# One change in four places of a fused attention and feed-forward kernel: convolution tiles, order of the attention's small products, composition schedule, seam

## The chip, the cores and the metric

The kernel runs on one core of one Trainium2 chip. It is written engine by engine (TensorE, VectorE, ScalarE, GpSimd and the DMA queues), with semaphores between them. The metric is the device time in microseconds, a median of runs. In the profile TensorE is PE (its weight loads PEld), VectorE DVE, ScalarE ACT, GpSimd POOL, SyncE SP.

## The reference, cut to what matters

The input has 8 sequences of 1024 tokens with 256 channels, all fp32. It goes through an attention encoder with a residual and a layer norm, then through a composed feed-forward part with a residual and a layer norm:

```
h = gelu(conv1d_grouped(x^T, conv1_w (1024,1,5), groups=256))      # 4 hidden channels each
h = conv1d_grouped(h, conv2_w (256,4,5), groups=256)^T
h = layernorm(h + x)
for i in range(4):                                                # 4 layers
    q = gelu(h Wq + bq) + 0.21;  k = gelu(h Wk + bk) + 0.21;  v = h Wv + bv
    q_r, k_r = rope(q), rope(k);  z = 1 / (q . mean(k))            # 16 heads of 16
    h = layernorm(q_r (k_r^T v / n) * z + h)
f = gelu(h W1 + b1) W2 + b2;  a = layernorm(f + h);  x = layernorm(x + a)
W1', W2' = sum over 32 chosen primitives of weight * A_k B_k       # top 32 of 64, softmax
out = layernorm(x + gelu_tanh(x W1') W2')
```

## The kernel before, in words

**Convolution (`conv_phase`, lines 57 to 376).** Four pairs of sequences times 8 channel groups are 32 steps. In step n TensorE runs `conv1(n)`, then `to_tokens(n - 2)` (transposes), then `conv2(n - 1)`. `conv1` (line 241) holds 32 fp32 products: 2 taps x 4 output slots `s` x 4 row groups `j`, each with 32 rows and 32 columns of the array and 512 moving columns; row group j writes PSUM bank `hid_ps[(4n + j) % 6]`, slot s its partitions 32s to 32s+31. Slots 0 and 1 take tap `second`, slots 2 and 3 tap `1 - second`. `conv2` (line 253) holds 8 products of 128 rows and 32 columns. ScalarE applies gelu (line 300), GpSimd copies edges (lines 185 to 187) and normalises an earlier pair, VectorE adds bias and input (line 322), keeps the turned rows (line 329) and measures them (`measure`). `prep` folds layer norm gains into the projection weights and biases: `prep.tensor` makes bias rows, `prep.tensor_columns` turns them into columns after ScalarE's `scalar_rows`, and `prep.vector_biases` finishes them. The last pair is normalised later, by `conv.last`, inside the first attention units.

**Attention (`attention_phase`).** 8 sequences x 4 layers are 32 units; unit n works on lane n % 4. TensorE's list for a unit, in order: `key_value(n-1)` (line 891, 128 rows by 32 columns), `project(n,0,"k",0)` (six fp32r products of 128x512), `turn_u(n,1)` (line 834, transposes of the second token half), `turn_kv(n-1)` (line 899, one product with the matrix `rot`), three more key projections, `turn_k` twice (line 854), `outputs(n-1)` (line 917, 32x32 tiles), `turn_k` twice, four query projections, `values` for four pairs of token tiles into `big[0..3]`, `turn_u(n+1,0)`, `denominators(n)` (line 876). What `turn_u` makes goes through ScalarE (`hT_hi`, line 956) and VectorE (`hT_lo`, line 1059), and the projections of that half wait for both. Projections, turned keys, denominators and key_value share four PSUM banks, `ring`, handed on in the order of `TURN`; `emptied_by` names the semaphore at which a bank comes free. GpSimd's list for a unit is `residual(n)` (it waits for `turn_u(n,1)`), an `invert` of an earlier unit, four `sum_k` and three rotations of q. VectorE copies the rotated kv (line 1145, `copy_turned`), measures unit n-2, rotates keys and finishes unit n-1.

**Composition (`compose_phase`).** 32 pairs of primitives ("duos", 16 per weight) are summed in PSUM. For pair n ScalarE makes the high parts (lines 1774, 1775), VectorE the low parts (lines 1804, 1806), TensorE multiplies. Three pairs are buffered (`SPLIT`), six raw loads (`RAW`). Between the pairs ScalarE and VectorE finish the last three attention units by a table written out by hand: `FINISH` (VectorE), `UNITS_AT` (ScalarE: four `unit` activations, before some of them `spread`, lines 1004 and 1005, after which GpSimd's `invert`, lines 797 and 799, runs), `FIRST_AT` (the first feed-forward weights), `TAKE_AT` (the finished weight 1 out of PSUM), `BIAS_AT`. The feed-forward part that follows (`ffn_phase`) is long and is not edited but for one more parameter.

Of the kernel before, what the change touches and what calls it, by code (L numbers as in the profile page):

```python
# [14 lines left out]
P = 128  # L15
# [28 lines left out]
def conv_phase(nc, x, bands1, bands2, conv1_b, conv2_b, eye, u0, comp, tri, w_col, picks, prep, keep, place, sems, stack,  # L44
# [5 lines left out]
    S = 4  # L50
# [13 lines left out]
    with ctx:  # L64
# [159 lines left out]

        def tensor(e, first):
            w = Waits(e)

            def conv1(n):
                l, cp = n // CP % 2, n % CP
                w.wait_ge(d_x[l][part_of(cp)], 16 * (n // CP // 2 + 1))  # L230
                w.wait_ge(d_band1[part_of(cp)], 2 * 16 if part_of(cp) else 16)

                for second in range(2):
                    for s in range(S):
                        k = second if s < 2 else 1 - second
                        for j in range(ROWS):
                            r = slice(32 * j, 32 * j + 32)
                            out = hid_of(n, j)[32 * s:32 * s + 32, :].rearrange("p (b g) -> p b g", b=2)
                            src = xs[l][r, cp, k:k + COLS].rearrange("p (b g) -> p b g", b=2)
                            w.wait_ge(s_hidden, ROWS * n + j - HID + 1)  # L240
                            m = e.matmul(out[:, :, second:], band1[r, cp, k, s, :], src[:, :, second:], start=not second,  # L241
                                         stop=bool(second))
                            if second and s == S - 1:
# [12 lines left out]

            def to_tokens(n):
                w.wait_ge(d_eye, 16)
                w.wait_ge(rank.s_v, rank.ROW + 1)
                w.wait_ge(s_convT, n + 1)  # L260
                w.wait_ge(s_y, n)
                for t in range(2 * MT):
                    m = e.transpose(back_ps[:, t, :], convT[:, n % 2, t * P:(t + 1) * P], identity[:, :])
                m.then_inc(s_back, 1)

            for n in range(STEPS + LAG):
                if n < STEPS:
                    conv1(n)
                if n == STEPS + LAG - 1:

                    w.wait_ge(s_hidden, ROWS * STEPS)
                    first()
                    prep.tensor(e)
                if 0 <= n - LAG < STEPS:
                    to_tokens(n - LAG)
                if 0 <= n - 1 < STEPS:
                    conv2(n - 1)
                if n == 1:
                    rank.tensor(e)
            prep.tensor_columns(e, identity)  # L280

# [32 lines left out]
        def vector(e, first):  # L314
# [17 lines left out]
            for n in range(STEPS + LAG):  # L332
# [3 lines left out]
                if n == STEPS + LAG - 1:  # L336
                    first()
                if 0 <= n - LAG < STEPS:
                    keep_rows(n - LAG)
# [5 lines left out]
                for layer in prep.due(n, 1):  # L345
                    prep.vector(e, layer)
            prep.vector_biases(e)

# [254 lines left out]
def attention_phase(nc, u_in, u_out, T, H, w_split, bias_qk, bias_v, keep, place, sems, stack, d_u0, d_u4, prefetch,  # L603
# [21 lines left out]
    with ctx:  # L625
# [64 lines left out]
        ring_of = lambda n, kind, b: ring[turn_of(n, kind, b) % RING]  # L690
        emptied_by = {"k": (s_gk, 4), "kt": (s_ks, 4), "q": (s_gq, 4), "den": (s_z, 1), "kv": (s_kvr, 1)}

# [123 lines left out]
        def tensor(e, then):  # L816
# [79 lines left out]
            def turn_kv(n):  # L896
                w.wait_ge(d_consts, 3 * 16)
                w.wait_ge(s_kvw, n + 1)
                e.matmul(ring_of(n, "kv", 0)[:, 2 * P:2 * P + CB * D], rot[:, :], kv[:, :, :].rearrange("p c n -> p (c n)"),
                         start=True, stop=True).then_inc(s_rot, 1)  # L900
# [18 lines left out]

            conv.tensor(e, lambda: turn_u(0, 0))  # L920
            for n in range(UNITS):
                if n >= 1:
                    key_value(n - 1)
                project(n, 0, "k", 0)
                turn_u(n, 1)
                if n >= 1:
                    turn_kv(n - 1)
                project(n, 0, "k", 1)
                project(n, 1, "k", 0)
                project(n, 1, "k", 1)  # L930
                turn_k(n, 0)
                turn_k(n, 1)
# [17 lines left out]
        def scalar(e, then):  # L950
# [87 lines left out]
            def last(g):  # L1038

                n = UNITS - 3 + g // 2  # L1040
                if g % 2 == 0 and n > UNITS - 3:
                    spread(n)
                for o in range(4 * (g % 2), 4 * (g % 2) + 4):
# [6 lines left out]

            then(e, last)

        def vector(e, then):
# [88 lines left out]
            def copy_turned(n):  # L1142
                w.wait_ge(s_rot, n + 1)
                w.wait_ge(s_out, n)
                e.tensor_copy(kv_rot[:, :, :].rearrange("p c n -> p (c n)"),
                              ring_of(n, "kv", 0)[:, 2 * P:2 * P + CB * D]).then_inc(s_kvr, 1)

# [10 lines left out]
            for n in range(UNITS):  # L1158
# [3 lines left out]
                split_u(n, 1)  # L1162
                if n >= 1:
                    copy_turned(n - 1)
                if n >= 2:
                    measure(n - 2, 0)
                    measure(n - 2, 1)
                if n == 0:
                    conv.last.vector(e, w, 0)
                    conv.last.vector(e, w, 1)  # L1170
                rotate_k(n, 0)
                k_mean(n)
                for u in range(1, DUOS):
                    if n == 0:
                        conv.last.vector(e, w, u + 1)
                    rotate_k(n, u)
# [5 lines left out]
                if n == 0:  # L1182
                    for half_group in range(5, 2 * conv.last.groups):
                        conv.last.vector(e, w, half_group)
# [25 lines left out]
def ffn_phase(nc, x, u_in, out, w1, b1, w2, rows2, comp, identity, w_col, picks, place, sems, before, early,  # L1210
# [12 lines left out]
    with ctx:  # L1223
# [238 lines left out]

        def scalar(e, last):
            w = Waits(e)
# [15 lines left out]

            compose.scalar(e, last, lambda: split_a(0, 0, 0))
            w.wait_ge(s_w_lo, 2)
# [194 lines left out]
def compose_phase(nc, up, down, comp, w_col, picks, place, sems, before, first, early, d_early):  # L1677
# [8 lines left out]
    with ctx:  # L1686
# [18 lines left out]
        FINISH = {2: 0, 4: 1, 5: 2, 6: 3, 7: 4, 9: 5, 10: 6, 11: 7, 12: 8, 13: 9, 15: 10}  # L1705
        UNITS_AT = {3: 0, 5: 1, 8: 2, 10: 3, 16: 4, 17: 5}

        FIRST_AT = {20: 0, 24: 1}
        TAKE_AT = DUOS + 6
        BIAS_AT = DUOS + 9  # L1710
        ROWS_AT = len(duos) - 3
# [50 lines left out]

        def scalar(e, last, rows):
            w = Waits(e)
# [19 lines left out]
            for n in range(len(duos)):  # L1784
                prepare(n)
                if n in UNITS_AT:
                    last(UNITS_AT[n])
                if n in FIRST_AT:
                    wait_free(w, before.free["all"])
                    first.scalar(e, FIRST_AT[n])  # L1790
# [266 lines left out]
```

## Time and profile before

| | us |
|---|---|
| runs, median (lowest to highest) | 1863.13 (1861.23 to 1863.57) |
| profiled execution, its own time | 1859.66 |
| its span | 1857.9 |

| engine | busy us | share of the span |
|---|---|---|
| PE | 1832.2 | 99% |
| PEld | 1528.6 | 82% |
| DVE | 1416.6 | 76% |
| ACT | 934.3 | 50% |
| POOL | 1011.6 | 54% |

The convolution fills about the first 163 us, the attention units the time to 1009.7, the composition that to 1109.9, the feed-forward part the rest. Matmuls are pipelined and overlap, so the time between the starts of two groups of products says more of TensorE than its busy share does. The granted clock is 0.998 of full speed over the span.

### The profile page before, as it was taken

Reading aid. Unit: us, or ns where it says so; the run is one execution under the profiler, and the core shown is the slowest. Engines: PE = TensorE matmul, PEld = TensorE weight load, DVE = VectorE, ACT = ScalarE, POOL = GpSimd, SP = SyncE. Lnnn points to the kernel's source line nnn. Section 1 sums busy time; section 2 is a strip of 40 time slices with the busy share of each in tenths; the row PEclk is TensorE's granted clock in tenths of the full one; section 3 lists DMA queues with packets and bytes.
Section 4 is the critical chain, followed back from the end, with each engine's and each line's share of the span. In section 5 each row is a group of like instructions: output and inputs, shape, how many; then the busy total and the mean of one; then the engine's idle time right before and its main releaser. Section 6 shows DMA issues by size and latency. Waiting matters only on the chain.

```text
span 1857.9 us, 50038 instructions
## 1 busy us (share of the span) xinstructions
PE 1832.2 (99%) x21188; PEld 1528.6 (82%) x21188; DVE 1416.6 (76%) x3329; ACT 934.3 (50%) x1741; POOL 1011.6 (54%) x775
## 2 busy tenths in 40 slices
PE   8999999999999999999999999999999999999998
PEld 2334888888888888888887799999999999999998
DVE  3556788888888888888887767777777777777777
ACT  4554667766676667766676653232323232323231
POOL 1455999899999999899996112222222222222221
PEclk9999999999999999999999999999999999999999
DMA  8354120010102110010104940010101010101000
GB/s 291 131 207 184 56 80 17 3 36 2 36 2 104 64 56 11 2 36 2 59 2 134 308 153 32 26 44 26 44 26 44 26 44 26 44 26 42 28 12 24
DMA packets 25249, 115.62 MB, mean 62 GB/s; under 512 B 4481, under 2 KB 5441, under 8 KB 19905
## 3 DMA queue, kind: packets, MB, share of 16 engines
q1 hardware_dynamic: 21104, 89.69, 13.7%
q0 software_dynamic: 1152, 12.58, 1.9%
q10 hardware_dynamic: 2768, 10.15, 1.4%
q8 instruction: 166, 2.72, 0.6%
q14 instruction: 59, 0.48, 0.1%
HBM read 80.95 MB, written 31.46 MB: 61 GB/s over the span
## 4 chain that ended last, share of the span: by engine, by line
PE 96%; DVE 2%; ACT 1%; issue 0%; DMA 0%; POOL 0%; SPq 0%; ACTq 0%; DVEq 0%; POOLq 0%
PE bankC L34 13%; PE bankC L33 13%; PE bankC L32 13%; PE ring L32 7%; PE ring L34 6%; PE ring L33 6%; PE big L917 5%; PE hid_ps L241 4%; PE big L34 3%; PE big L32 3%; PE big L33 3%; PE conv_ps L253 3%; PE ring L854 3%; PE big L834 3%; PE ring L891 2%; PE ring L876 2%
## 5 line engine op out<-in xcount | busy, mean ns | idle before, releaser
L32 PE MATMUL bankC<-down_hi,act_hi 128*128 128x256 f32 x1024 | 291.4, 285 | 0.0
L34 PE MATMUL bankC<-down_hi,act_lo 128*128 128x256 f32 x1024 | 289.6, 283 | 0.0
L33 PE MATMUL bankC<-down_lo,act_hi 128*128 128x256 f32 x1024 | 288.6, 282 | 0.0
L1553 DVE TENSOR_TENSOR act_lo<-gel,act_hi 128x512 fp32r<-128x512 f32 x256 | 210.9, 824 | 8.7
L34 PE MATMUL bankC<-aT_hi,up_lo 128*128 128x512 f32 x512 | 199.7, 390 | 0.0
L33 PE MATMUL bankC<-aT_lo,up_hi 128*128 128x512 f32 x512 | 199.5, 390 | 0.0
L32 PE MATMUL bankC<-aT_hi,up_hi 128*128 128x512 f32 x512 | 199.4, 389 | 0.0
L32 PEld LDWEIGHTS bankC<-down_hi,act_hi 128*128 128x128 f32 x1024 | 193.8, 189 | 1.2
L33 PEld LDWEIGHTS bankC<-down_lo,act_hi 128*128 128x128 f32 x1024 | 193.2, 189 | 1.4
L1507 POOL TENSOR_TENSOR hC<-hC,vecC 128x1024 f32<-128x1024 f32 x16 | 38.5, 2404 | 284.5 <-PE turn L1406 284.5
L34 PEld LDWEIGHTS bankC<-down_hi,act_lo 128*128 128x128 f32 x1024 | 193.2, 189 | 0.0
L1513 POOL TENSOR_TENSOR rstdC<-var_epsC,minus_halfC 128x4 f32<-128x4 f32 x47 | 52.8, 1123 | 254.1 <-DVE var_epsC L1578 254.1
L1059 DVE TENSOR_TENSOR hT_lo<-big,hT_hi 128x512 fp32r<-128x512 f32 x128 | 82.4, 686 | 109.0 <-ACT hT_hi L956 109.0
L762 POOL TENSOR_TENSOR kr<-kr,kc 128x512 f32<-128x512 f32 x128 | 161.7, 1297 | 0.0
L1478 ACT ACTIVATE gel<-bankC,b1s 128x512 f32<-128x512 f32 x128 | 88.4, 690 | 140.5 <-PE bankC L34 140.4
L1478 ACT ACTIVATE gel<-bankC 128x512 f32<-128x512 f32 x128 | 76.6, 599 | 155.5 <-PE bankC L34 155.5
L781 POOL TENSOR_TENSOR yB<-yB,shift 128x1024 f32<-128x1024 f32 x64 | 151.0, 2383 | 0.0
L1470 ACT ACTIVATE aT_hi<-turn 128x512 fp32r<-128x512 f32 x64 | 34.8, 596 | 217.1 <-PE turn L1406 217.1
L778 POOL TENSOR_TENSOR yB<-yB,gain 128x1024 f32<-128x1024 f32 x48 | 114.4, 2404 | 52.4 <-PE big L834 52.4
L996 ACT ACTIVATE yB<-yB,offset,rstdB 128x256 f32<-128x256 f32 x256 | 129.4, 588 | 5.5 <-POOL offset L799 5.5
L788 POOL TENSOR_TENSOR qc<-gT,cos_q 128x512 f32<-128x512 f32 x96 | 124.3, 1295 | 0.0
L789 POOL TENSOR_TENSOR qs<-gT,sin_q 128x512 f32<-128x512 f32 x96 | 123.6, 1288 | 0.0
(205 smaller groups left out, 5252.1 us busy)
## 6 DMA issues: line engine op xcount, KB each, us to landing
raw_late<-in_AB SPq DMA_DIRECT2D x30, 320.0 KB, 3.9
u<-hA SPq DMA_DIRECT2D x8, 1024.0 KB, 4.6
u_next<-u SPq DMA_DIRECT2D x8, 1024.0 KB, 4.8
hC<-u SPq DMA_DIRECT2D x16, 512.0 KB, 3.9
xC<-in_x SPq DMA_DIRECT2D x16, 512.0 KB, 4.8
out<-w_flat SPq DMA_DIRECT2D x15, 512.0 KB, 2.6
w_flat<-in_AB SPq DMA_DIRECT2D x22, 320.0 KB, 3.7
w_split<-w_parts ACTq DMA_DIRECT2D x4, 1536.0 KB, 5.3
```

The costliest lines, as they stand in the source:

```text
L32: e.matmul(out, wh, xh, start=start, stop=False)
L33: e.matmul(out, wh, xl, start=False, stop=False)
L34: return e.matmul(out, wl, xh, start=False, stop=stop)
L762: e.tensor_tensor(kr[:, u, :], kr[:, u, :], kc[:, u, :], ALU.add).then_inc(s_kr, 1)
L778: e.tensor_tensor(tiles(y, a), tiles(src, a), row(gain), ALU.mult).then_inc(s_mul, 1)
L781: e.tensor_tensor(tiles(y, a), tiles(y, a), row(shift), ALU.add).then_inc(s_res, 1)
L788: e.tensor_tensor(qc[:, db, cols], gT[:, db, cols], table_q(cos_q, db, x), ALU.mult)
L789: e.tensor_tensor(qs[:, db, cols], gT[:, db, cols], table_q(sin_q, db, x), ALU.mult).then_inc(s_qr, 1)
L917: m = e.matmul(out, wt[ch, db, :], quarter(q[ch, db, :], j), start=q is qc, stop=q is qs)
L996: e.activation(y[:, o, :], y[:, o, :], ACT.Identity, bias=offset[:, two, o:o + 1], scale=rstd[:, two, o:o + 1]).then_inc(s_unit, 1)
L1478: e.activation(gel[:, n % GEL, :], bank_of(i, k, s, fb)[:, :], ACT.Gelu if k == 0 else ACT.Gelu_apprx_tanh, bias=b1s[:, fb:fb + 1] if k == ...
L1553: e.tensor_tensor(a_lo[:, fb, :], g, a_hi[:, fb, :].bitcast(F32), ALU.subtract).then_inc(s_act_lo, 1)
```

## The change: what it does

- The first convolution uses 32x64 tiles: two neighbouring slots in one product of 64 columns, so 16 products per step instead of 32.
- In an attention unit `turn_u(n,1)` goes ahead of all four key projections and `turn_kv(n-1)` behind them. `turn_kv` writes `big[0]` instead of the ring bank, and that bank comes free at `s_kvw` instead of `s_kvr`. VectorE's `copy_turned` goes behind the two measurements of unit n-2.
- At the end of the convolution TensorE also turns the second half of unit 0 (`second`) and makes the bias columns before the last `to_tokens`; VectorE's biases move ahead of the last `keep_rows`. In unit 0 the measurements of the last convolution rows, but for the first two, go behind the rotated keys.
- In the composition `spread` is separate from `unit` (`SPREAD_AT`, after pairs 6 and 16; before, it ran after pairs 8 and 16 directly ahead of the units), the last two groups of units move from pairs 16 and 17 to 18 and 19, the first feed-forward weights from 20 and 24 to 22 and 25, take and bias one pair later.

```diff
-                    for s in range(S):
-                        k = second if s < 2 else 1 - second
+                    for half in range(2):
+                        k = 1 - second if half else second
                         for j in range(ROWS):
...
-                            out = hid_of(n, j)[32 * s:32 * s + 32, :].rearrange("p (b g) -> p b g", b=2)
+                            out = hid_of(n, j)[rows, :].rearrange("p (b g) -> p b g", b=2)
...
+                            bands = band1[r, cp, k, 2 * half:2 * half + 2, :].rearrange("p s c -> p (s c)")
...
-                            m = e.matmul(out[:, :, second:], band1[r, cp, k, s, :], src[:, :, second:], start=not second,
-                                         stop=bool(second))
+                            m = e.matmul(out[:, :, second:], bands, src[:, :, second:], start=not second, stop=bool(second))
@@ end of the convolution, TensorE
                     first()
                     prep.tensor(e)
+                    second()
+                    prep.tensor_columns(e, identity)
...
-            prep.tensor_columns(e, identity)
@@ end of the convolution, VectorE
                     first()
+                    prep.vector_biases(e)
...
-            prep.vector_biases(e)
@@ attention, ring and turn_kv
-        emptied_by = {..., "kv": (s_kvr, 1)}
+        emptied_by = {..., "kv": (s_kvw, 1)}
...
-                e.matmul(ring_of(n, "kv", 0)[:, 2 * P:2 * P + CB * D], rot[:, :], ...)
+                if n + 1 < UNITS:
+                    w.wait_ge(s_lo, 4 * (n + 1) + 2)
+                else:
+                    w.wait_ge(s_vs, 4 * n + 4)
+                e.matmul(big[0][:, 0:CB * D], rot[:, :], ...)
@@ attention, TensorE's list
-            conv.tensor(e, lambda: turn_u(0, 0))
+            conv.tensor(e, lambda: turn_u(0, 0), lambda: turn_u(0, 1))
             for n in range(UNITS):
                 if n >= 1:
                     key_value(n - 1)
+                    turn_u(n, 1)
                 project(n, 0, "k", 0)
-                turn_u(n, 1)
-                if n >= 1:
-                    turn_kv(n - 1)
                 project(n, 0, "k", 1)
                 project(n, 1, "k", 0)
                 project(n, 1, "k", 1)
+                if n >= 1:
+                    turn_kv(n - 1)
@@ attention, VectorE's list
-                if n >= 1:
-                    copy_turned(n - 1)
                 if n >= 2:
                     measure(n - 2, 0)
                     measure(n - 2, 1)
+                if n >= 1:
+                    copy_turned(n - 1)
...
-                    if n == 0:
-                        conv.last.vector(e, w, u + 1)
...
-                    for half_group in range(5, 2 * conv.last.groups):
+                    for half_group in range(2, 2 * conv.last.groups):
@@ composition
-        UNITS_AT = {3: 0, 5: 1, 8: 2, 10: 3, 16: 4, 17: 5}
-        FIRST_AT = {20: 0, 24: 1}
-        TAKE_AT = DUOS + 6
-        BIAS_AT = DUOS + 9
+        UNITS_AT = {3: 0, 5: 1, 8: 2, 10: 3, 18: 4, 19: 5}
+        SPREAD_AT = {6: 0, 16: 1}
+        FIRST_AT = {22: 0, 25: 1}
+        TAKE_AT = DUOS + 7
+        BIAS_AT = DUOS + 10
```

## Rows read from the trace of the kernel before

**Rows 1.** The page, part 1: busy us (share of the span), instructions.
```profile
PE 1832.2 (99%) x21188; PEld 1528.6 (82%) x21188; DVE 1416.6 (76%) x3329; ACT 934.3 (50%) x1741; POOL 1011.6 (54%) x775
```
**Rows 2.** The page, part 4: the chain that ended last, by engine.
```profile
PE 96%; DVE 2%; ACT 1%; issue 0%; DMA 0%; POOL 0%; SPq 0%; ACTq 0%; DVEq 0%; POOLq 0%
```
**Rows 3.** Timeline, matmuls, one convolution step: start us, us, engine, line, operation, tiles, count.
```profile
103.28 2.35 PE L241 MATMUL hid_ps<-xs,band 32*32 32x512 f32 x64
105.55 0.66 PE L263 MATMUL back_ps<-identity,convT 128*128 128x128 f32 x4
106.14 1.93 PE L253 MATMUL conv_ps<-hidden,band 128*32 128x512 f32 x16
```
**Rows 4.** Timeline, weight loads of the same step, with [idle before <-releaser].
```profile
103.27 0.25 PEld L241 LDWEIGHTS hid_ps<-xs,band 32*32 32x32 f32 x32 [0.84 <-ACT hidden L300]
103.73 0.10 PEld L241 LDWEIGHTS hid_ps<-xs,band 32*32 32x32 f32 x1 [0.21 <-issue]
104.16 0.55 PEld L241 LDWEIGHTS hid_ps<-xs,band 32*32 32x32 f32 x31 [0.32 <-issue]
...
106.59 0.13 PEld L253 LDWEIGHTS conv_ps<-hidden,band 128*32 128x32 f32 x4 [0.30 <-issue]
107.02 0.13 PEld L253 LDWEIGHTS conv_ps<-hidden,band 128*32 128x32 f32 x4 [0.30 <-issue]
107.99 0.25 PEld L241 LDWEIGHTS hid_ps<-xs,band 32*32 32x32 f32 x32 [0.84 <-issue]
```
**Rows 5.** Four convolution steps: us, then PE, PEld, DVE, ACT, POOL busy, clock, DMA.
```profile
103.30:122.20 18.90, 18.90 (x348) 6.66 (x348) 11.95 (x30) 9.71 (x17) 12.70 (x20) 1.00 0.68 269
```
**Rows 6.** Timeline, matmuls, one attention unit.
```profile
482.89 0.51 PE L32 MATMUL ring<-hT_hi,w_second 128*128 128x512 f32 x1
...
484.39 1.04 PE L834 MATMUL big<-identity,yB 128*128 128x128 f32 x8
...
485.41 0.48 PE L32 MATMUL ring<-hT_hi,w_second 128*128 128x512 f32 x1
...
486.66 0.40 PE L34 MATMUL ring<-hT_hi,w_second 128*128 128x512 f32 x1
487.10 0.47 PE L32 MATMUL ring<-hT_hi,w_second 128*128 128x512 f32 x1
...
489.97 1.03 PE L854 MATMUL ring<-identity,gkT 128*128 128x128 f32 x8
...
494.47 0.48 PE L32 MATMUL ring<-hT_hi,w_second 128*128 128x512 f32 x1
...
500.13 0.28 PE L32 MATMUL big<-w_second,hT_hi 128*128 128x256 f32 x1
```
**Rows 7.** Waits of the weight loads, 228 to 1002 us: us, times, longest.
```profile
PEld ring L32 <- issue: 13.1, 29, 0.5
```
**Rows 8.** Busy time by engine, one attention unit (columns as in rows 5).
```profile
455.55:481.56 26.01, 25.97 (x406) 21.96 (x402) 21.56 (x51) 17.91 (x37) 23.74 (x17) 1.00 0.01 2
```
**Rows 9.** Timeline, matmuls, from the convolution's end through unit 0.
```profile
169.52 0.47 PE L32 MATMUL ring<-hT_hi,w_first 128*128 128x512 f32 x1 [0.64 <-issue]
...
178.58 0.50 PE L32 MATMUL ring<-hT_hi,w_first 128*128 128x512 f32 x1
...
180.90 0.50 PE L32 MATMUL ring<-hT_hi,w_first 128*128 128x512 f32 x1 [0.66 <-DVE kr L1071]
...
187.20 0.28 PE L32 MATMUL big<-w_first,hT_hi 128*128 128x256 f32 x1
```
**Rows 10.** Timeline, weight loads and ScalarE, composition.
```profile
1035.86 0.19 PEld L32 LDWEIGHTS acc<-duo_hi 128*128 128x128 f32 x1 [1.83 <-DVE duo_lo L1806]
...
1060.94 0.19 PEld L32 LDWEIGHTS acc<-duo_hi 128*128 128x128 f32 x1 [1.94 <-DVE duo_lo L1806]
1065.10 0.19 PEld L32 LDWEIGHTS acc<-duo_hi 128*128 128x128 f32 x1 [1.23 <-DVE duo_lo L1806]
...
1055.80 2.08 ACT L996 ACTIVATE yB<-yB,offset,rstdB 128x256 f32<-128x256 f32 x4 [2.89 <-POOL offset L799]
```

More of the change, by code:

```diff
@@ L223, in token_tile, with tensor @@
             return y[q % 2][:, g, :, :].rearrange("p a (j s c) -> p (a j) s c", j=ROWS, s=S)[:, :, s, :]
-        def tensor(e, first):
+        def tensor(e, first, second):
             w = Waits(e)
@@ L233, in conv1 @@
                 for second in range(2):
-                    for s in range(S):
-                        k = second if s < 2 else 1 - second
+                    for half in range(2):
+                        k = 1 - second if half else second
                         for j in range(ROWS):
-                            r = slice(32 * j, 32 * j + 32)
-                            out = hid_of(n, j)[32 * s:32 * s + 32, :].rearrange("p (b g) -> p b g", b=2)
+                            r, rows = slice(32 * j, 32 * j + 32), slice(64 * half, 64 * half + 64)
+                            out = hid_of(n, j)[rows, :].rearrange("p (b g) -> p b g", b=2)
                             src = xs[l][r, cp, k:k + COLS].rearrange("p (b g) -> p b g", b=2)
+                            bands = band1[r, cp, k, 2 * half:2 * half + 2, :].rearrange("p s c -> p (s c)")
                             w.wait_ge(s_hidden, ROWS * n + j - HID + 1)
-                            m = e.matmul(out[:, :, second:], band1[r, cp, k, s, :], src[:, :, second:], start=not second,
-                                         stop=bool(second))
-                            if second and s == S - 1:
+                            m = e.matmul(out[:, :, second:], bands, src[:, :, second:], start=not second, stop=bool(second))
+                            if second and half:
                                 m.then_inc(s_hid, 1)
@@ L690, in attention_phase @@
         ring_of = lambda n, kind, b: ring[turn_of(n, kind, b) % RING]
-        emptied_by = {"k": (s_gk, 4), "kt": (s_ks, 4), "q": (s_gq, 4), "den": (s_z, 1), "kv": (s_kvr, 1)}
+        emptied_by = {"k": (s_gk, 4), "kt": (s_ks, 4), "q": (s_gq, 4), "den": (s_z, 1), "kv": (s_kvw, 1)}
         def ring_empty(n, kind, b):
@@ L898, in turn_kv @@
                 w.wait_ge(s_kvw, n + 1)
-                e.matmul(ring_of(n, "kv", 0)[:, 2 * P:2 * P + CB * D], rot[:, :], kv[:, :, :].rearrange("p c n -> p (c n)"),
+                if n + 1 < UNITS:
+                    w.wait_ge(s_lo, 4 * (n + 1) + 2)
+                else:
+                    w.wait_ge(s_vs, 4 * n + 4)
+                e.matmul(big[0][:, 0:CB * D], rot[:, :], kv[:, :, :].rearrange("p c n -> p (c n)"),
                          start=True, stop=True).then_inc(s_rot, 1)
@@ L1040, in last @@
                 n = UNITS - 3 + g // 2
-                if g % 2 == 0 and n > UNITS - 3:
-                    spread(n)
                 for o in range(4 * (g % 2), 4 * (g % 2) + 4):
@@ L1049, in last @@
                     e.dma_start(rows_of(u_out, b), y_of(n)[:, :, :]).then_inc(d_sent[b % 2], 16)
-            then(e, last)
+            then(e, last, lambda g: spread(UNITS - 2 + g))
         def vector(e, then):
@@ L1145, in copy_turned @@
                 e.tensor_copy(kv_rot[:, :, :].rearrange("p c n -> p (c n)"),
-                              ring_of(n, "kv", 0)[:, 2 * P:2 * P + CB * D]).then_inc(s_kvr, 1)
+                              big[0][:, 0:CB * D]).then_inc(s_kvr, 1)
             FINISH = [[(turn, 0)], [(turn, 1), (scale, 0)], [(add_h, 0), (turn, 2)], [(scale, 1), (add_h, 1)],
@@ L1461, in tensor, with scalar @@
                         down_product(i, k, s, following)
-        def scalar(e, last):
+        def scalar(e, last, spread):
             w = Waits(e)
@@ L1479, in gelu @@
                                  bias=b1s[:, fb:fb + 1] if k == 0 else 0.0).then_inc(s_gelu, 1)
-            compose.scalar(e, last, lambda: split_a(0, 0, 0))
+            compose.scalar(e, last, spread, lambda: split_a(0, 0, 0))
             w.wait_ge(s_w_lo, 2)
@@ L1761, in tensor, with scalar @@
                     rows()
-        def scalar(e, last, rows):
+        def scalar(e, last, spread, rows):
             w = Waits(e)
@@ L1787, in scalar @@
                     last(UNITS_AT[n])
+                if n in SPREAD_AT:
+                    spread(SPREAD_AT[n])
                 if n in FIRST_AT:
```

## The prediction

> **What bounds the kernel now.** I read the page first: TensorE has something in flight for 99% of the span [rows 1], and the chain that ended last runs through its products for 96% [rows 2]. The time is therefore TensorE's own list of instructions, plus the few places where it stands still. So each edit is worth what it takes out of TensorE's order of time. A busy share of 99% hides this, because products overlap; I read starts, not busy time: the timeline of one convolution step [rows 3, 4], of one attention unit [rows 6], of the seam between both [rows 9] and of the composition sums [rows 10]. The other engines were read only for their room: in a convolution stretch of 18.9 us DVE is busy 11.95, ScalarE 9.71 and GpSimd 12.70 [rows 5]; in an attention unit of 26.01 us DVE has 21.56, ScalarE 17.91 and GpSimd 23.74 [rows 8]. GpSimd is the nearest to becoming the bound, with 2.3 us to spare per unit.
>
> **First convolution, 32x64 tiles.** It runs 32 times. Every fp32 product shows up as two matmul instructions, each with a weight load, so a step has 64 + 64 instructions now and 32 + 32 after. From rows 3 a step goes 103.28 (first convolution), 105.55 (turning), 106.14 (second convolution), and the next first convolution is at 107.99 (the window in rows 4 ends there): 2.27 + 0.59 + 1.85 = 4.71 us.
> Per tile of the array nothing changes in count: 16 tiles with 4 passes each become 8 tiles with 4 passes each, because a product of 64 columns takes the place of two of 32. Four passes on a tile have a price in the trace: the second convolution, 4 column tiles with 4 passes each, takes 1.85, and its weight loads come 0.43 us apart (106.59, 107.02), which is a pass [rows 4]. The first convolution needs 2.27 for the same 4 passes. Its loads say where the 0.42 goes: 32 loads start together (two passes for 16 tiles), one more comes at 103.73, and then none until 104.16, after which 31 come within 0.55 us. 32 loads with 32 products is all that is in flight, and the third pass of 15 of the tiles starts only after that stand. I take it that TensorE can hold no more than 16 such products at once; the new step has 16 in all, so the stand has no cause left. New step: 1.85 plus some 0.03 for four more tiles, 1.88; the gain is 0.39. For the 30 steps after the two that wait for the first loads this is 11.7, and I allow 0.5 for those two: 12.2 us.
> Bounds. The trace has no 64-column tile. Best: four passes of 0.43 without a tail over the second convolution's, gain 0.42, 13.4 us. Worst within this mechanism: the stand stays, 0. Below zero, see the rivals. I stay at 0.39, since the second convolution is the nearest row. Cover: ScalarE needs 4 activations per step and the helpers 11.95 and 12.70 of 18.9 us for four steps [rows 5]; with steps of 4.32 four of them give 17.3. A step in which GpSimd also prepares weights can be late by some tenths, once per layer.
> The Trainium skill, "TensorE: Matmul & The Clock Gate", section "LDWEIGHTS (loading the stationary operand)", says that loading takes columns / 1.2 ns, whatever the rows, so 64 columns would load for 27 ns more than 32. By that rule, if loads were not hidden, four passes would lose 0.11 per step and the term would be 8.8 instead of 12.2 (an estimate from that page). Against it speaks that in the second convolution loads are issued a whole pass ahead [rows 4]; I don't subtract it.
>
> **Attention: turning moved ahead of the four key projections, the rotation behind them.** Now a unit has one projection (482.89 to 484.39, 1.50), the turning, the rotation, and three projections (485.41 to 489.97, 4.56) [rows 6]: 6.06 for 24 products. Within the second block the start at 487.10 comes 0.44 after that at 486.66, where 0.23 is the usual step, and the product behind it is late too: about 0.29 in all. It is the wait for the turned half: turned at 485.2, copied by ScalarE, subtracted by DVE, wanted two projections on. The same stand of the weight loads shows in 29 units, 13.1 us, 0.45 each [rows 7]. In the new order the turning stands in front of all four, so that its copies have two projections (2.8 us) of cover where they now have one. Four projections in one block have a price: the query projections, 494.47 to 500.13, 5.66 [rows 6] (5.56 in about half of the units). So 6.06 becomes 5.56 to 5.66, gain 0.40 to 0.50, I take 0.45: the wait (0.29) and one re-entry into the projections from another kind of product (0.16). Everything else of the unit is only moved. 31 units: 14.0 us.
> What is queued behind the moved steps: the rotation waits for key_value on DVE, done some 5 us earlier now; its copy on DVE moves behind the two measurements, and has 1.1 us until the outputs want it (two turnings of keys, 0.96, lie between). The rotation now writes big0, long read at that point and refilled only by the outputs. The ring bank of key_value comes free with its masked sums, so the fourth projection has nothing to wait for. GpSimd's residual starts 1.5 us earlier in the unit; a unit of 25.56 still leaves it 1.8 us [rows 8]. Bounds: if the wait reappears, 0.16 x 31 = 5.0; best 0.50 x 31 = 15.5.
> The Trainium skill, "TensorEngine Tiling (Array Packing)", section "Key Properties", says that changing the tiling mode drains TensorE, not a change of tile. All products that this edit regroups use the whole array, so by that rule no drain goes and only the wait is won: 0.29 x 31 = 9.0, total 28.9 instead of 33.9. The trace disagrees in part: 24 products take 5.66 in one block, and 6.06 less the 0.29 of the wait, 5.77, in two [rows 6].
>
> **The seam and the first unit.** The query projections of unit 0 go from 178.58 to 187.20, 8.62 us [rows 9], where 5.56 to 5.66 is their price [rows 6]: 3.0 lost to stands like the one at 180.90, waiting for DVE's rotated keys, because DVE has measurements of the last convolution rows between them. The change puts these behind the rotated keys. The 0.64 in front of 169.52 is the wait for the biases, which now come two steps earlier, and the key projections win what they win in every unit, 0.45. Together 4.1. What is late next: I leave 0.5 us, for the first rotated key and ScalarE's last key half. Gain 3.6. The price: GpSimd gets the later measurements later, so its sums of keys end about as now while key_value is wanted 3.6 us sooner; by my count of its timeline about 1 us is left. Bounds: 1.5 (GpSimd late) to 4.1.
>
> **Composition.** TensorE stands three times for DVE's low parts: 1.83, 1.94 and 1.23 [rows 10], and 0.27 once more; 5.1 us with late second products. Cause: ScalarE waits for GpSimd's power between spread and units (2.89 us ahead of 1055.80 [rows 10], and much the same once before), with the next pair's high parts queued behind. Spread now comes two pairs ahead, so the power runs while ScalarE prepares, and both its waits go. What is late next: ScalarE's units at pairs 18 and 19, first at 22, take at 23, first at 25. Counting ScalarE 1.55 per pair, 2.1 per four units, 2.2, 2.0 and 1.9 for the rest against TensorE's 2.88 per pair, DVE hands over pair 24 0.4 to 2 us late. I take 1.0: gain 4.1; bounds 2.5 and 5.1.
>
> **Sum.** 12.2 + 14.0 + 3.6 + 4.1 = 33.9. The feed-forward part has no edit. The profiled execution took 1859.66 us (span 1857.9 and 1.8 around it): 1825.8. The median of the runs is 3.5 above that execution, so as a median I say 1829.
>
> **Rivals.**
> A. The first convolution keeps its 2.27: what it stands for isn't the number in flight but something per tile (each tile still gets four passes and four loads). For it: 15 tiles are late together, which a per-tile cost could also show. Against: the second convolution's tiles don't pay it. 33.9 - 12.2 = 21.7, 1841. Chance 0.12.
> B. The wait in the attention unit moves: DVE's key_value, the inversion and the split now meet, and the third projection, or the outputs behind the later copy, wait again for 0.29 or so. 14.0 becomes 5.0: 1838. For it: DVE is 83% busy. Against: after the move the half is ready about 0.8 us before it is wanted. 0.10.
> C. Seam and composition give back their gain, because helpers that had been excused by TensorE's stands become the bound: 1829 + 6 = 1835. 0.07.
> D. Slower: two 64-column halves of the array don't run beside each other in this form. Eight passes in a row of 0.43 and a tail of 0.13 make 3.6 per step, 1.3 more than now, 42 us in 32 steps; less the other 21.7, +21: 1884. It decides from 0.68 us per step upward. For it: no 64-column product is in the trace. Against: four 32-column ones at once are. 0.03.
>
> **How the numbers follow.** Forecast 0.68, A 0.12, B 0.10, C 0.07, D 0.03. The forecast's own range from the bounds is 1823 to 1836; up to 1841 it takes in C, B and A's value, and leaves out D and the ends. About 0.2% (3.7 us) is what a measurement can tell from no change. Faster 0.96, same 0.01, slower 0.03.
>
> **What would show it.** Right: one first convolution of 32 products from start to the turning in 1.85 to 1.92, loads 0.43 apart, no stand; 24 projections in one block in 5.56 to 5.66 and a unit of 25.5 to 25.6; query projections of unit 0 in under 6.1; at most one stand near pair 24. Wrong: a first convolution over 2.2; a stand in front of the third key projection; GpSimd with no idle time in the units.

## The result

The changed kernel takes 1848.76 us (median of 4 runs, 1846.09 to 1849.74) against 1863.13; the ratio is 0.9921, 95% interval 0.9909 to 0.9934. It is faster, by 14.4 us where 34 were forecast, and above the 1841 up to which the prediction took in its rivals (its own bounds were 1823 to 1836). The profiled executions differ by as much: 1859.66 before, 1846.09 after, 13.6 us. By stretches of TensorE's timeline, each from the start of its first product to the start of the next stretch's (the first from the start of the span, the last to the end of its last product):

| stretch | before | after | gained | predicted |
|---|---|---|---|---|
| convolution, to the first turning | 163.28 | 153.53 | 9.75 | 12.2 |
| seam and unit 0, to key_value of unit 0 | 31.53 | 28.52 | 3.0 | 3.6 |
| attention, to the first composition product | 814.85 | 817.49 | -2.6 | 14.0 |
| composition, to the first feed-forward product | 100.27 | 96.76 | 3.5 | 4.1 |
| feed-forward part | 742.4 | 742.4 | 0 | 0 |

So nearly all of the miss is in the attention. The page of the changed kernel, part 1, hides it as that of before did [rows 1]:

```profile
PE 1815.4 (98%) x20164; PEld 1526.6 (83%) x20164; DVE 1416.5 (77%) x3329; ACT 937.6 (51%) x1741; POOL 1011.5 (55%) x775
```

Its chain by engine (part 4) has only one new thing against [rows 2], "issue" at 1%:

```profile
PE 96%; DVE 1%; issue 1%; ACT 1%; DMA 0%; POOL 0%; SPq 0%; DVEq 0%; ACTq 0%; POOLq 0%
```

**Convolution.** Timeline of the matmuls of one step, after, and below it the weight loads of the next first convolution (columns as in rows 3 and 4):

```profile
99.46 0.65 PE L263 MATMUL back_ps<-identity,convT 128*128 128x128 f32 x4
100.05 1.93 PE L253 MATMUL conv_ps<-hidden,band 128*32 128x512 f32 x16
101.90 1.97 PE L242 MATMUL hid_ps<-xs,band 32*64 32x512 f32 x32
103.80 0.66 PE L263 MATMUL back_ps<-identity,convT 128*128 128x128 f32 x4
```

```profile
101.90 0.23 PEld L242 LDWEIGHTS hid_ps<-xs,band 32*64 32x64 f32 x16 [0.84 <-issue]
102.38 0.18 PEld L242 LDWEIGHTS hid_ps<-xs,band 32*64 32x64 f32 x8 [0.25 <-issue]
102.81 0.18 PEld L242 LDWEIGHTS hid_ps<-xs,band 32*64 32x64 f32 x8 [0.25 <-issue]
```

From 101.90 to 103.80 the first convolution takes 1.90 where it took 2.27 [rows 3]. 16 loads start together (two passes for the 8 tiles), then 8 more every 0.43 us, with no stand as at 103.73 before [rows 4].

**A normal attention unit** is what was forecast. Busy time of one, after (columns as in rows 5), against 26.01 in [rows 8]:

```profile
441.86:467.45 25.59, 25.59 (x426) 22.05 (x416) 21.58 (x51) 18.03 (x37) 24.07 (x17) 1.00 0.01 2
```

and the wait that the edit was priced by is gone. Waits of the weight loads, 153 to 1000 us (us, times, longest), against 13.1 in 29 units [rows 7]; the first line is new:

```profile
PEld big L923 <- issue: 19.3, 43, 2.7
...
PEld ring L32 <- issue: 1.9, 3, 1.3
```

L923 is `outputs`: 128 short products (256 instructions with their loads) that take 2.38 us from first to last. In ten of the units TensorE stands once inside them, for nothing that the profile shows. Here the unit at 345 us, matmuls of the changed kernel, the stand at the end:

```profile
345.08 0.27 PE L905 MATMUL big<-kv,rot 128*128 128x64 f32 x1
345.19 1.04 PE L855 MATMUL ring<-identity,gkT 128*128 128x128 f32 x8
346.16 0.71 PE L923 MATMUL big<-qc,kv 32*32 32x256 f32 x32
...
347.70 0.59 PE L923 MATMUL big<-qc,kv 32*32 32x256 f32 x14
349.35 0.72 PE L923 MATMUL big<-qs,kv_rot 32*32 32x256 f32 x31 [1.06 <-issue]
```

Product 97 of 128 starts at 347.9 and the next one at 349.35. No semaphore is waited for inside `outputs`, and kv_rot, the last thing that they need, was copied at 345.39 (the row of DVE in the same kernel):

```profile
345.39 0.22 DVE L1149 COPY kv_rot<-big 128x64 f32<-128x64 f32 x1 [1.06 <-PE big L905]
```

What does happen in that time is a transfer. DMA queues of the changed kernel, 346.7 to 348.2 us; there is no other packet from 343 to 349.4:

```profile
DMA packets 1, 0.02 MB, mean 11 GB/s; under 512 B 0, under 2 KB 0, under 8 KB 0
## 3 DMA queue, kind: packets, MB, share of 16 engines
q8 instruction: 1, 0.02, 5.9%
```

In the page, queue q8 has 159 such packets of 16.4 KB together (2.61 MB), for 40328 instructions of TensorE: some 254 to a packet. It is TensorE's own program, brought while it runs. This packet takes 1.4 us and ends at 348.14; 1.2 us later the products go on. In all ten stands they go on 1.2 to 1.6 us after the packet's end.

In the kernel before, the copy and the start of the outputs lie further apart (unit at 465 us, DVE and matmuls):

```profile
460.85 0.21 DVE L1145 COPY kv_rot<-ring 128x64 f32<-128x64 f32 x1
```

```profile
464.86 0.71 PE L917 MATMUL big<-qc,kv 32*32 32x256 f32 x32
```

**Theory T1.** TensorE's sequencer, the part that reads the program and hands its instructions on, runs ahead of the array and asks for the next packet when it comes near the end of what it has. In the kernel before the copy of kv_rot ends 3.8 us ahead of the outputs, the sequencer runs into them early, and where a packet's border falls in them the packet is fetched 1.1 to 2.8 us before they start. In the changed kernel the copy ends 0.55 us before the outputs. Their wait for it is met in time for the data, but it holds the sequencer until then; the packet is asked for when the outputs already run (it starts 0.5 to 0.7 us into them, in unit 18 2.5 us), and 256 instructions in 2.4 us are through before it is usable. The border slides by 21 products per unit, so two units in about six have it in the late part of the outputs: 6, 7, 12, 13, 18, 19, 24, 25, 30 and 31.

**Rival R1.** The rotation in big[0], or the products packed more closely around it, make the stands. Any account that looks only at when data is ready belongs here.

### The profile page after: what moved, and what is told of

It reads as the page before. It is cut to its first block, busy times and chain, and to the rows that moved or that the text cites. A ratio compares the mean times of both kernels' runs of the same rounds, so it can differ in the third digit from the quotient of the medians.

```text
span 1844.3 us, 48020 instructions
## 1 busy us (share of the span) xinstructions
PE 1815.4 (98%) x20164; PEld 1526.6 (83%) x20164; DVE 1416.5 (77%) x3329; ACT 937.6 (51%) x1741; POOL 1011.5 (55%) x775
## 3 DMA queue, kind: packets, MB, share of 16 engines
q8 instruction: 159, 2.61, 0.6%
## 4 chain that ended last, share of the span: by engine, by line
PE 96%; DVE 1%; issue 1%; ACT 1%; DMA 0%; POOL 0%; SPq 0%; DVEq 0%; ACTq 0%; POOLq 0%
PE bankC L34 13%; PE bankC L32 13%; PE bankC L33 13%; PE ring L32 6%; PE ring L34 6%; PE ring L33 6%; PE big L923 5%; PE ring L855 3%; PE big L34 3%; PE big L32 3%; PE big L33 3%; PE big L835 3%; PE hid_ps L242 3%; PE conv_ps L253 3%; PE ring L892 2%; PE ring L877 2%
## 5 line engine op out<-in xcount | busy, mean ns | idle before, releaser
L971 ACT ACTIVATE gkT<-ring,bias_qk 128x512 f32<-128x512 f32 x128 | 88.3, 690 | 81.1 <-PE ring L34 81.1
```

Source lines behind the costliest of these rows:

```text
L971: e.activation(gkT[:, db, half(x)], ring_of(n, "k", 2 * x + db)[:, :], ACT.Gelu, bias=bias_qk[:, at:at + 1], accum_out=k_sums[:, db, x:x + ...
```

## The experiments

**1. The wait alone, in the kernel before.** The outputs wait for one thing more, which DVE ends 0.7 us before they start:

```
                 w.wait_ge(s_kvr, n + 1)
                 if n + 1 < UNITS:
+                    w.wait_ge(s_mom, 8 * n)
                     w.wait_ge(s_lo, 4 * (n + 1) + 4)
```

> The kernel before with one wait more at the head of the outputs, for the end of the measurements of the unit before, which DVE ends 0.6 us before the first output product; no work, order or bank changes. T1: the wait is met in time for the data but holds TensorE's sequencer up to 0.6 us before the outputs, so stands of 0.7 to 2.6 us appear inside the outputs in the two or three units of every six in which a packet is fetched there (around units 6, 12 or 13, 18 or 19, 24 or 25, 30 or 31), 12 to 17 us in all: 1876 us (1872 to 1882). Rival R1 (bank or spacing of the products) and any theory that looks at data alone: the wait costs nothing, 1863 us (within 1.5).

1875.84 us (1873.42 to 1878.21), ratio to before 1.0062, interval 1.0045 to 1.0078. The wait is met by the measurements' last row at 363.63, the outputs start at 364.32, and still:

```profile
364.32 0.71 PE L918 MATMUL big<-qc,kv 32*32 32x256 f32 x32
...
365.86 0.59 PE L918 MATMUL big<-qc,kv 32*32 32x256 f32 x14
367.06 0.72 PE L918 MATMUL big<-qs,kv_rot 32*32 32x256 f32 x31 [0.61 <-issue]
```

Stands came in units 6, 7, 12, 13, 18, 19, 24, 25, 30 and 31, the same ten. In the profiled run the outputs are 10.3 us longer in sum and the attention stretch 12.1. In this kernel rotation, banks and order are those of before, so the stands need nothing of what R1 names: a wait that delays no data makes them, and the kernel is 12.3 us slower than the runs of the kernel before beside it (1863.51). Two differences outside the attention are not the wait's doing: this trace's seam is 2.2 us longer, as is that of experiment 6, although neither edits it, and its composition 3.0, with 6.8 us at half clock. The attention stretch is therefore the cleaner figure.

**2. The rotation early again, in the changed kernel.**

```
                 project(n, 0, "k", 1)
+                if n >= 1:
+                    turn_kv(n - 1)
                 project(n, 1, "k", 0)
                 project(n, 1, "k", 1)
-                if n >= 1:
-                    turn_kv(n - 1)
 ...
+                if n >= 1:
+                    copy_turned(n - 1)
                 if n >= 2:
                     measure(n - 2, 0)
                     measure(n - 2, 1)
-                if n >= 1:
-                    copy_turned(n - 1)
```

> The changed kernel with one thing back: the rotation is issued after the second key projection instead of after the fourth, and its copy stands before the two measurements on DVE. turn_u, the ring's early release and big[0] stay as in the change. Theory T1 (TensorE's own program comes in packets by DMA; the late copy holds TensorE's sequencer at the head of the outputs, so in the units where a packet's border falls in them the packet is asked for too late and the 128 short products run dry): with the copy done some 3 us before the outputs the sequencer runs ahead again and the 11 stands inside the outputs go, the outputs take 2.38 us in every unit, and the time is 1833 us (1831 to 1836). Rival R1 (the stands come from rotation and outputs sharing big[0], or from the products of the outputs standing closer behind the transposes): big[0] and the order of the short products stay, so the stands stay and the time is 1848 us (within 2).

1835.22 us (1834.62 to 1836.21), ratio 0.9848, interval 0.9831 to 0.9864. The outputs take 2.38 us in every unit of this trace. The same unit as above, matmuls, DVE, and the DMA queues from 344.2 to 345.4:

```profile
341.76 0.33 PE L905 MATMUL big<-kv,rot 128*128 128x64 f32 x2
344.78 1.04 PE L855 MATMUL ring<-identity,gkT 128*128 128x128 f32 x8
345.75 0.71 PE L923 MATMUL big<-qc,kv 32*32 32x256 f32 x32
```

```profile
342.13 0.22 DVE L1149 COPY kv_rot<-big 128x64 f32<-128x64 f32 x1 [1.42 <-PE big L905]
```

```profile
DMA packets 1, 0.02 MB, mean 14 GB/s; under 512 B 0, under 2 KB 0, under 8 KB 0
## 3 DMA queue, kind: packets, MB, share of 16 engines
q8 instruction: 1, 0.02, 5.0%
```

The packet is now on its way before the outputs' first product at 345.75, not in the middle of them. That big[0] is used did no harm, and with experiment 1 R1 falls. One cost of the same kind is left: behind the last outputs TensorE stands until 987.95, 1.3 us after the end of a packet, so the last unit is 1.5 us longer than before. There the copy ends only 0.46 us ahead.

**3. A dose between the two.** Rotation as in 2, but the copy left behind the measurements: it ends 1.7 us ahead of the outputs (0.55 in the change, 3.4 in 2).

> The changed kernel with the rotation behind the second key projection, but its copy left where the change has it, behind the two measurements: DVE then copies as soon as the measurements end, some 1.0 us earlier than in the change (1.55 us before the outputs instead of 0.55). T1 gives a dose: packets are asked for 1.0 us earlier, so stands of 0.70 us go, those of 1.44 shrink to some 0.4, the one of 2.64 to some 1.6: outputs 3 to 5 us above their undisturbed sum instead of 12.7, and the time is 1839 us (1836 to 1842). If what counts is whether the rotation stands next to the outputs, as in early, 1835 us; if what counts is the copy's place behind the measurements, 1848 us.

1837.36 us (1834.92 to 1838.49), outputs 2.8 us above their sum without stands; 1.6 of it lie in units 1 to 31 and the rest in the last outputs, just under the 3 to 5 that I expected. Two stands are left of ten, in units 18 and 19; that of unit 18 shrank from 2.64 between two products to 1.19. Its row in the changed kernel, and in this one:

```profile
637.10 1.07 PE L923 MATMUL big<-qs,kv_rot 32*32 32x256 f32 x8 [2.26 <-issue]
```

```profile
634.00 0.63 PE L923 MATMUL big<-qs,kv_rot 32*32 32x256 f32 x8 [0.81 <-issue]
```

Unit 18 is the worst in both. One of the kernel's own transfers of u, 1 MB, runs just then, and in the changed kernel the program's packet started 2.46 us into the outputs there, against 0.5 to 0.7 elsewhere. After that stand, in the changed kernel, the granted clock was 0.5 for 3.4 us.

The traces also give the distance that T1 rests on. In the ten units of the changed kernel, of experiment 1 and of this one the packet starts 1.0 to 1.3 us after the wait at the head of the outputs was met, whether that is 0.55, 0.7 or 1.7 us ahead of them; only unit 18 (2.6 to 3.0) and, in this experiment, unit 19 (1.7) are later. So the packet moves with the wait. What inside the sequencer makes it ask just then no trace shows.

**4. The border moved.** 92 waits on a semaphore long met, once, before the units:

```
+            for _ in range(92):
+                e.wait_ge(d_w[0], 16)
             for n in range(UNITS):
```

> The changed kernel with 92 waits more on TensorE, all long met, issued once ahead of the first attention unit: nothing changes in the units but which instruction of theirs falls on a packet's border. A unit takes 46 instructions more than three packets of 256, so 92 more move the borders by two units. T1: the stands inside the outputs move two units earlier, to units 4 and 5, 10 and 11, 16 and 17, 22 and 23, 28 and 29, with about the same sum, and the time stays near 1849 us plus what the 92 waits cost once (0 to 5 us). A rival that ties the stands to anything in data, batches or DMA traffic of the kernel: they stay in units 6/7, 12/13, 18/19, 24/25, 30/31.

1853.54 us (1851.92 to 1854.84), ratio 0.9945. In the traces it is 7.0 us longer than the changed kernel, 3.4 of them in the seam, where the 92 waits stand and the clock was at one half for 3.4 us. The stands moved, to units 5 and 6, 11 and 12, 17 and 18, 23 and 24, 29 and 30, with one more in the last outputs: one unit earlier, not two. The trace says why: it holds 48066 instructions against 48020, so the 92 waits became 46 instructions, or 23 products, and a unit slides the border by 21. My "46 instructions more than three packets" for a unit was wrong by the same reading; it is 42. Unit 5, which ran undisturbed in the changed kernel, now has the border 12 products from its end:

```profile
299.91 0.89 PE L923 MATMUL big<-qs,kv_rot 32*32 32x256 f32 x17
301.40 0.65 PE L923 MATMUL big<-qs,kv_rot 32*32 32x256 f32 x12 [0.60 <-issue]
```

So the stands follow the program's position and not batch, layer or data.

**5. All but the attention edit.**

> The changed kernel without its attention edit (order of turn_u, rotation and copy, ring release as before): tiles of the convolution, seam and composition alone. From the two traces these three gave 9.75, 3.0 and 3.5 us: 1863.1 - 16.3 = 1847 us (1845 to 1849), so the attention edit is worth nothing or a loss of 2 us beside them. Rival (the stands are caused by the conv edit's shift of the program against the packets, not by the attention edit): the stands are here too, inside the outputs, and the time is 1860 us.

1844.91 us (1843.61 to 1846.85), attention 814.61 as before (814.85), no stand. The edit that was to bring 14.0 us costs about 4 beside the other three (2.9 in the attention stretch of the two traces).

**6. The attention edit alone, on the kernel before.**

> The kernel before with the attention edit alone (turn_u ahead of the key projections from unit 1 on, rotation behind them into big[0], its copy behind the measurements, ring bank freed at kvw). T1: the products of a unit run as in the changed kernel, so the stands inside the outputs come with it, in two of every six units; the gain of the grouping (0.45 us x 31 = 14.0) and the stands (12 to 17) cancel: 1864 us (1861 to 1868). Had the stands needed the other parts of the change, 1849 us.

1870.51 us (1867.77 to 1875.36), ratio 1.0047, interval 1.003 to 1.0064: slower than before, and 2.5 above the end of what I expected. To the same ten units comes unit 1, where the border fell at product 95 and TensorE stood for 3.35 us; the granted clock fell to one half towards the end of that stand, for 6.8 us:

```profile
211.47 0.58 PE L922 MATMUL big<-qc,kv 32*32 32x256 f32 x1 [2.98 <-issue]
```

**7. The convolution's tiles alone.**

> The kernel before with the first convolution's products in 32x64 tiles and nothing else. T3 (30 of the 32 steps give 0.38 us, the first two wait for loads, two steps wait for DVE and give 0.9 back): the first turn_u starts 9.5 to 10 us earlier and the time is 1853.5 us (1852 to 1855). The rival that the loss of 2.4 us against the predicted 12.2 came from the seam's edits: 1851 us.

1853.53 us (1850.75 to 1853.64), ratio 0.9938. First turning at 153.66 where the changed kernel has 153.53: the 2.4 us that the convolution stayed behind its forecast are its own. Its composition, without the edit of it, took 103.4: the stands of before and 6.8 us at half clock.

**8. Rotation directly behind the turning**, copy before the measurements, and key_value ahead of the inversion on DVE, to keep the 24 key products in one block:

> The changed kernel with the rotation directly behind turn_u, ahead of all key projections, its copy ahead of the measurements, and on DVE key_value ahead of invert so that the rotation need not wait. Early splits the 24 key products and pays 5.82 us for what takes 5.56 + 0.17 in the changed kernel, so 0.1 to 0.15 us in each of 31 units come back if the rotation doesn't wait for kvw: 1832 us (1830 to 1835). If DVE's kv is late, PE stands 0.3 to 0.6 us in each unit ahead of the rotation: 1845 to 1853 us. No stands inside the outputs either way.

1838.84 us (1836.06 to 1842.05): a miss of the 1832 expected, and 3.6 us above experiment 2. No stand inside the outputs of units 1 to 31, but the turning and the rotation take 0.93 and 0.22 instead of 0.85 and 0.14, as much as the split block costs, some units lose another 0.5 there, the last outputs have a stand of 1.7, and the composition, 98.8, has 6.8 us at half clock.

**9. The bias products in four lots.** In the changed kernel 32 one-column products stand in one lot of 3.49 us, from 1076.00, and the clock falls afterwards. Theory T2: the lot is what lowers the clock. Busy time in two windows, the first up to 1.4 us into the lot, the second behind it (the clock is the third figure from the end):

```profile
1073.90:1077.40 3.50, 3.50 (x33) 3.50 (x32) 1.73 (x3) 2.08 (x4) 0.00 (x0) 1.00 0.00 0
1080.90:1084.30 3.40, 3.40 (x19) 3.40 (x18) 0.46 (x2) 0.44 (x1) 0.00 (x0) 0.50 0.93 264
```

```
-                if n == BIAS_AT:
+                if BIAS_AT - 3 <= n <= BIAS_AT:
                     w.wait_ge(s_out_lo, 4)
-                    first.tensor_bias(e, acc[0][0])
+                    first.tensor_bias(e, acc[0][0], n - BIAS_AT + 3)
```

> As rot_first, and the 32 one-column bias products of the composition in four lots of 8, behind its blocks 23 to 26, instead of in one lot of 3.5 us behind block 26. Theory T2 (the half clock of 3.4 us after that lot, in the traces of the changed kernel, early, no_attention and after_shift, comes from the lot and costs 1.4 to 1.9 us): the granted clock stays 1.00 through the composition and the time is 1.6 us under rot_first. Rival: the lot's own 3.5 us grow with the splits and the clock was chance: same as rot_first within 0.5, clock still halved somewhere in the composition.

1837.76 us (1836.67 to 1838.88) beside 1838.84, a difference that these runs don't resolve; the whole composition at full clock in the profiled run:

```profile
991.16:1086.87 95.71, 95.25 (x625) 87.37 (x621) 70.61 (x113) 61.18 (x95) 11.23 (x9) 1.00 0.76 255
```

**10. Both, 2 and 9, with 2 again on the same chip.**

> Early (rotation behind the second key projection, copy ahead of the measurements) and the bias products of the composition in four lots of 8. T1 and T2 add: no stand inside the outputs, clock 1.00 through the composition, which takes 95.7 us from its first product to the first of the feed-forward part instead of 96.9: 1834 us (1833 to 1836). If the lot's halved clock was chance, the time is early's, 1835.2.

> Early once more, beside early_bias on the same chip, for the difference of the two: 1835 us, 1 to 1.5 us above early_bias by T2, equal to it by chance alone.

1833.86 us (1832.76 to 1840.15), ratio 0.9838, interval 0.9825 to 0.9852, and 1835.16 (1833.99 to 1835.44), 0.9842, 0.9829 to 0.9856. The first is the fastest version here, 29 us under the kernel before and 15 under the changed one; its difference to the second is not resolved. In its profiled run, the 1840.15, the clock fell in the composition all the same:

```profile
989.20:1090.11 100.91, 97.56 (x625) 89.69 (x621) 72.31 (x113) 61.07 (x95) 11.73 (x9) 0.97 0.73 241
```

This fall has a neighbour of its own. It came at 1083.8, 15 us behind the last lot, in a stand of TensorE of 3.35 us, for which ScalarE had waited 3.8 us for a load of `w_flat` (matmuls of experiment 10):

```profile
1084.82 0.58 PE L32 MATMUL acc<-duo_hi 128*128 128x256 f32 x1 [3.35 <-DVE duo_lo L1812]
```

Eleven traces have the products in one lot, and in nine of them the clock falls inside the lot or up to 1.6 us behind it (experiments 1 and 7, with the composition of before, among them); the kernel before and experiment 6 have no fall. Neither trace with four lots has a fall beside one. So T2 has more for it than against it, but it stays open: the one lot doesn't decide alone, and two traces without it are few. What goes with a fall is measured: a composition of 96.8 to 97.4 us where the one without is 95.7, beside 3.4 us at half clock, and 3.0 or 3.1 us more beside 6.8 (103.2 and 103.4 against 100.3; 98.8 against 95.7).

## Why the prediction was wrong

**Attention, 14.0, measured -2.6. This is the failed step**, and in it the sentence on the copy: it "has 1.1 us until the outputs want it", and before it "Everything else of the unit is only moved". The slack was right (the rotation starts 1.1 us ahead of the outputs, its copy ends 0.55 ahead) and the wrong thing to count. A wait that is met before its data is wanted still fixes how early the sequencer can be in what follows, and what follows is a dense stretch, 256 instructions in 2.4 us. Rival B had the right place, "the outputs behind the later copy", but as a wait for data of 0.29 a unit; none of the waits is one for data. The outputs are 12.7 us longer in sum, and some 2.4 more lie around the stands: unit 18 is 3.96 us longer than before, of which its outputs are 3.0 and the half clock most of the rest, and the last unit 0.9. The price of the gain itself held: the third projection's wait is gone, 24 products in 5.56 to 5.66, and the undisturbed units are 0.24 to 0.46 shorter (one 0.69; unit 17, next to the transfer of u, gained nothing), 0.40 on average, against the 0.45 forecast. 31 times 0.40, less 12.7 and 2.4, is about the -2.6 measured. Without stands, experiment 2 gets 9.1 of the 14.0, as it pays 0.1 per unit for two blocks of 12 again (2.83 and 2.85 us, and 0.14 for the rotation, against 5.56 and 0.17), and a last unit 1.5 us longer.

The Trainium skill, "Perfetto Trace Analysis", section "Per-instruction lifecycle: what the profiler-reported window actually captures", has instructions of 64 bytes and puts their fetch in the sequencer ahead of any wait. The first agrees with the trace here (16.4 KB for some 254 instructions, 65 bytes each); that the fetch can itself be late, the runs here show and that section does not say.

**Convolution, 12.2, measured 9.75.** The gain per step was right: 1.90 against 1.88, and loads in lots of 8, 0.43 apart. The stand went with half the products in flight, as forecast; that their number is its cause no run tests by itself. The size was off at the ends. From the fourth step on the stretch is 10.0 us shorter (140.22 to 130.21) instead of 11.7: two steps, 19 and 27 counted from 0, take 0.43 and 0.48 longer, in waits for DVE; I had allowed "some tenths, once per layer" and not subtracted it. The first three steps gave nothing, since the loads from memory set them (the fourth first convolution starts at 23.1 to 24.8 us in all kernels). The 0.11 per step that I weighed for loading 64 columns shows in 0.02 at most. Rivals A and D fell with this.

**Seam, 3.6, measured 3.0.** The query projections of unit 0 went from 8.62 to 5.57 us. What was "late next" was neither of the two that I named but the low half of the turned input, at the third key projection; matmuls of the changed kernel:

```profile
160.20 0.47 PE L32 MATMUL ring<-hT_hi,w_first 128*128 128x512 f32 x1 [0.15 <-issue]
...
164.05 0.47 PE L32 MATMUL ring<-hT_hi,w_first 128*128 128x512 f32 x1 [0.86 <-DVE hT_lo L1063]
```

**Composition, 4.1, measured 3.5.** The stands, 5.1 us, shrank to 0.35, better than the 1.0 that I left; the clock at one half for 3.4 us took back some 1.1 to 1.7 (experiment 10). A fall of the clock was no term of the sum. Rival C didn't come: seam and composition kept 6.5 of their 7.7 us.

**The chances.** 0.96 for faster was right. The range was too narrow because every bound came from rows about data and engines; a cost of the instruction stream had no row to be seen in, as it was hidden in every unit of the kernel before.

## What to carry to other kernels

Before moving a producer closer to its consumer, look at what follows the wait on the waiting engine: if it is a dense run of short instructions (here 256 in 2.4 us), the wait has to be met well ahead of it. Here 3.4 us ahead was enough, 1.7 us left two stands of ten, and a slack of 0.55 us in data left all ten. A stand in the middle of such a run, with "issue" as its releaser and one packet on the instruction queue beside it, is this case; that it sits in some of many equal units, with a period, gives it away. Take such a stand as a reason to let the wait come earlier, not to look for the missing data.

## What the runs showed of the hardware

TensorE's program comes in packets of 16.4 KB while the kernel runs; one mostly takes 0.9 to 1.5 us on its queue (the longest 1.9), it starts 1.0 to 1.3 us after a late wait is met, and in the ten stands the products went on 1.2 to 1.6 us after its end. The kernel's own transfers can hold it up: beside one of 1 MB it was asked for or started 1.9 us later, though no run moves such a transfer alone. 92 semaphore waits in a row took 46 instructions of that program (experiment 4), while the one more wait per unit of experiment 1 took one each (30 waits, 50068 instructions in the trace against 50038). And the granted clock fell to one half for 3.4 or 6.8 us behind three of the four longest stands (2.64, 3.35 and 3.38 us; not behind one of 2.62), at or just behind the one lot of one-column products in nine of eleven traces, without any long stand there, and once in a stand of 3.35 us for a late load. It also fell for 3.4 us about the last unit's outputs in the traces of experiments 3 and 10, which nothing here explains.
